# Marks issued with the similarity, self weights added on the diagonal, and SiLU as one ACT function in a two-stage image kernel

## The reference, cut to what matters

```python
xn  = xf / max(norm(xf), 1e-12)
sim = einsum('bnc,bmc->bnm', xn, xn)
val, idx = top_k(sim, 9)                       # the token itself is one of the nine
v   = val / (val.sum(-1) + 1e-06)
gcn = lambda feat, w, b: einsum('bnkc,bnk->bnc', (feat @ w)[idx], v) + b
out = silu(group_norm(gcn(xn, w1, b1)))        # 4 groups
out = silu(group_norm(gcn(out, w2, b2)))
x   = x + out
```

## Time and profile before

| | us |
|---|---|
| median of three runs | 780.92 |
| lowest, highest | 778.73, 781.6 |
| the profiled execution | 778.75 |
| its span, first to last instruction | 777.0 |
| PE busy | 663.6 (85%) |
| DVE busy | 574.1 (74%) |
| POOL busy | 483.0 (62%) |
| ACT busy | 353.3 (45%) |

### The profile page before, as it was taken

The page is one execution under the profiler, slowest core; times in us unless marked ns, Lnnn a source line. Parts: engine busy times, 40 slices in busy tenths (PEclk is TensorE's granted clock), DMA queues, the critical chain, the costliest instruction groups (busy, mean ns, idle before and its releaser), DMA issues.

```text
span 777.0 us, 11257 instructions
## 1 busy us (share of the span) xinstructions
PE 663.6 (85%) x3632; PEld 299.1 (38%) x3632; DVE 574.1 (74%) x1086; ACT 353.3 (45%) x578; POOL 483.0 (62%) x536
## 2 busy tenths in 40 slices
PE   3476869999999999999999999999999999787764
PEld 2353434444343434343434434343434343332221
DVE  2235678888888888888888878888888888866411
ACT  2234436364546555564546454646446454424110
POOL 0122665859596768676776849676767677674600
PEclk9557679999999999999999999999999999988776
DMA  2003242434343442524253434334353424333300
GB/s 68 1 14 56 54 96 54 96 57 95 82 96 68 81 97 56 121 57 109 56 95 68 96 69 96 77 81 88 64 106 64 90 60 83 74 83 75 69 14 14
DMA packets 148731, 55.93 MB, mean 72 GB/s; under 512 B 138017, under 2 KB 138273, under 8 KB 148673
## 3 DMA queue, kind: packets, MB, share of 16 engines
q1 hardware_dynamic: 148672, 55.21, 34.6%
HBM read 13.11 MB, written 4.33 MB: 22 GB/s over the span
## 4 chain that ended last, share of the span: by engine, by line
PE 51%; DVE 18%; issue 16%; POOL 8%; ACT 3%; DMA 2%; SPq 0%; POOLq 0%; ACTq 0%; DVEq 0%
PE pC L798 25%; PE pS L755 9%; DVE mask L603 5%; POOL rn L319 3%; DVE y L627 3%; PE pC L818 2%; PE pB L775 2%; PE pA L673 2%; POOL st_g L297 2%; DVE top L585 2%; PE pA L712 2%; PE pB L701 2%; PE pS L763 2%; ACT pB L464 1%; DVE st_g L497 1%
## 5 line engine op out<-in xcount | busy, mean ns | idle before, releaser
L798 PE MATMUL pC<-adj,xt 128*64 128x512 f32 x1024 | 265.4, 625 | 3.6 <-POOL adj L347 2.8
L585 DVE MAX8 top<-pS 128x8 f32<-128x1024 f32 x128 | 156.8, 1225 | 37.8 <-PE pS L763 36.6
L444 ACT COPY adj<-pS 128x1024 f32<-128x1024 f32 x128 | 129.2, 1009 | 95.1 <-PE pS L755 95.0
L347 POOL TENSOR_TENSOR adj<-maskT,adj 128x128 f32<-128x128 f16 (+7 forms) x128 | 164.4, 1285 | 11.7
L755 PE MATMUL pS<-xn 64*128 64x512 f32 x256 | 153.3, 682 | 10.9 <-DVE mask L603 5.7
L603 DVE MATCH_REPLACE8 mask<-top,pS 128x1024 uint16<-128x1024 f32 x128 | 155.4, 1214 | 0.0
L755 PE MATMUL pS<-xn,xsw 64*128 64x512 f32 x256 | 153.5, 682 | 2.0 <-DVE mask L603 1.8
L337 POOL TENSOR_TENSOR adj<-maskT,adj 128x128 f32<-128x128 f16 (+6 forms) x112 | 130.4, 1165 | 0.0
L798 PEld LDWEIGHTS pC<-adj,xt 128*64 128x64 f32 x1024 | 59.7, 139 | 88.8 <-issue 70.1
L319 POOL TENSOR_TENSOR rn<-ssq,minus_half 128x8 f32<-128x8 f32 x16 | 26.5, 1656 | 49.7 <-DVE selfsim L573 49.7
L613 DVE TENSOR_TENSOR g<-pC,vbc 128x512 f32<-128x512 f32 x32 | 22.1, 692 | 42.5 <-PE pC L798 42.5
(11 more groups left out here) (120 smaller groups left out, 1035.2 us busy)
## 6 DMA issues: line engine op xcount, KB each, us to landing
xs<-x SPq DMA_DIRECT2D x32, 128.0 KB, 2.8
rbc<-rn_row SPq DMA_DIRECT2D x32, 128.0 KB, 2.9
xsw<-xn SPq DMA_DIRECT2D x32, 128.0 KB, 2.5
vbc<-v_row SPq DMA_DIRECT2D x32, 128.0 KB, 2.9
out<-res SPq DMA_DIRECT2D x32, 128.0 KB, 2.4
maskT<-mask SPq DMA_TRANSPOSE x128, 3.1
cst<-packed SPq DMA_DIRECT2D x1, 453.5 KB, 3.5
rn_row<-rnT SPq DMA_DIRECT2D x16, 4.0 KB
```

The costliest lines, as they stand in the source:

```text
L347: pool.tensor_tensor(above, m[:, r, 0:r + 1, :].bitcast(F16), above, ALU.mult).then_inc(done["upper"], 1)
L444: act.copy(adj[b % 2][:, r, :], pS[r % 2][:, :]).then_inc(done["sim_copied"], 1)
L585: dve.max(top[:, r, :], pS[r % 2][:, :]).then_inc(done["tile_top"], 1)
L798: mm = pe.matmul(pC[h * C:(h + 1) * C, :], xt[:, t % NJ, t // NJ, :], adj[b % 2][:, t, h * H:(h + 1) * H], start=(t == 0), stop=(t == NT - 1))
```

## The change

- The two mark matmuls of a block stand directly behind its two similarity matmuls and in the same step; `marks` is gone as a stage. ACT copies the marked similarities, and MAX waits for the copy.
- The select on the diagonal is gone. The mask is zero there, so `upper` clears the diagonal, and POOL then adds `selves`, a diagonal of the tokens' own similarities, which ACT makes for each block from `ident` (new stage `itself`).
- `top` has ten columns: the eight largest, the own similarity and the small number. One reduce sums them. It is double-buffered.
- SiLU is one ACTIVATE with the function Silu, which writes `y2` or `y3` itself. `zh`, Tanh, L627 and the halved constants are gone, and with them Tanh's use of pB.
- The statistics of `g1` and `g2` use pB in place of pC. Their two matmuls stay.
- A new table of times, with a list `BEGINS` in place of `PERIOD`, sets another order on all queues.

```diff
-PERIOD = 41.68
+BEGINS = [0, 39.7423, 79.6495, 119.4031, 159.2975, 198.9522, 238.8737, 278.5581, 318.3809, 358.0611, 397.9632, 437.6484,
...
-                    live += [(b * PERIOD + at, steps) for at in TIMES[engine][stage.__name__]]
+                    live += [(BEGINS[b] + at, steps) for at in TIMES[engine][stage.__name__]]
...
-                    own = m[:, r, r, :].bitcast(F16)
-                    pool.affine_select(out=own, in_=own, compare_op=ALU.not_equal, fill=1.0, base=0, pattern=[[-1, P]],
-                                       channel_multiplier=1).then_inc(done["diagonal"], 1)
-                    if r == 0:
-                        pool.wait_ge(*of_tile("sim_copied", n))
-                    pool.wait_ge(*of_tile("diagonal", n))
+                    pool.wait_ge(*of_tile("sim_copied", n))
                     above = a[:, 0:r + 1, r * P:(r + 1) * P]
                     pool.tensor_tensor(above, m[:, r, 0:r + 1, :].bitcast(F16), above, ALU.mult).then_inc(done["upper"], 1)
+                    yield
+
+                    pool.wait_ge(*of_tile("upper", n))
+                    pool.wait_ge(*of_tile("self_ready", n))
+                    own = a[:, r, r * P:(r + 1) * P]
+                    pool.tensor_tensor(own, own, selves[:, r, :], ALU.add).then_inc(done["diagonal"], 1)
 
...
+            def itself(b):
+                for r in range(NT):
+                    yield
+                    act.wait_ge(*of("ss_read", b, 2))
+                    act.wait_ge(*of_tile("diagonal", NT * (b - 1) + r))
...
-            def silu_parts(b, tag, src, half):
+            def silu(b, tag, src, dst, signal):
                 yield
                 act.wait_ge(*of(f"{tag}_bias", b))
...
-                act.activation(pB[:, :], src[:, :], ACT.Tanh, bias=st[tag][:, 15:16],
...
+                if tag == "g1":
+                    act.wait_ge(*of("xt2_ps", b - 1))
+                else:
+                    act.wait_ge(*of("res_ready", b - 1))
+                act.activation(dst[:, :], src[:, :], ACT.Silu, bias=st[tag][:, 15:16], scale=st[tag][:, 14:15]).then_inc(done[signal], 1)
...
+                dve.wait_ge(*of("self_ready", b - 2, NT))
+                dve.wait_ge(*of("v_tot", b - 2))
 
                 dve.wait_ge(*of("ss_ps", b))
                 dve.tensor_scalar(ssq[:, :], pB[:, 0:NT], 1e-24, 1.0 / SSCALE, ALU.max, ALU.mult).then_inc(done["ss_read"], 1)
-                dve.tensor_scalar(selfsim[b % 2][:, :], pB[:, 0:NT], SSCALE * 1e24, SSCALE, ALU.mult, ALU.min).then_inc(done["ss_read"], 1)
+                dve.tensor_scalar(top[b % 2][:, :, TOP], pB[:, 0:NT], SSCALE * 1e24, SSCALE, ALU.mult, ALU.min).then_inc(done["ss_read"], 1)
...
-                    dve.wait_ge(*of_tile("marked", n))
-                    dve.wait_ge(*of("v_sum", b - 1))
-                    dve.max(top[:, r, :], pS[r % 2][:, :]).then_inc(done["tile_top"], 1)
+                    dve.wait_ge(*of_tile("sim_copied", n))
+                    dve.wait_ge(*of("v_tot", b - 2))
+                    dve.max(top[b % 2][:, r, 0:TOP], pS[r % 2][:, :]).then_inc(done["tile_top"], 1)
                 yield
                 dve.wait_ge(*of("tile_top", b, NT))
-                dve.tensor_reduce(vsum[:, :], top[:, :, :], AX.X, ALU.add).then_inc(done["v_sum"], 1)
-                dve.wait_ge(*of("v_sum", b))
                 dve.wait_ge(*of("ss_read", b, 2))
-                dve.scalar_tensor_tensor(out=vtot[:, :], in0=vsum[:, :], scalar=1e-6 * SSCALE, in1=selfsim[b % 2][:, :],
-                                         op0=ALU.add, op1=ALU.add).then_inc(done["v_tot"], 1)
...
-                variance(b, tag, pC)
-                yield
-                affine(b, tag, halved[:, first_const:first_const + 1], halved[:, first_const + 1:first_const + 2])
-                yield
-                dve.wait_ge(*of(f"{tag}_tanh", b))
-                if tag == "g1":
-                    dve.wait_ge(*of("xt2_ps", b - 1))
-                else:
-                    dve.wait_ge(*of("res_ready", b - 1))
-                dve.scalar_tensor_tensor(out=act_out[:, :], in0=pB[:, :], scalar=1.0, in1=half[:, :], op0=ALU.add,
-                                         op1=ALU.mult).then_inc(done[act_name], 1)
+                variance(b, tag, pB)
+                yield
+                affine(b, tag, const(weight), const(shift))
...
-                    mm = pe.matmul(pS[r % 2][:, h * H:(h + 1) * H], src[b % 2][c, rows], xn[b % 2][c, :], start=True, stop=True)
-                mm.then_inc(done["sim_ps"], 1)
-
-            def mark(b, r):
-                n = NT * b + r
-                own, _ = token_block(r)
-                pe.wait_ge(*of_tile("sim_copied", n))
+                    pe.matmul(pS[r % 2][:, h * H:(h + 1) * H], src[b % 2][c, rows], xn[b % 2][c, :], start=True, stop=True)
                 for s in range(2):
                     mm = pe.matmul(pS[r % 2][:, r * P + s * C:r * P + (s + 1) * C], place16[own, s, :], mark16[own, :], start=False,
                                    stop=True, skip_group_check=True)
-                mm.then_inc(done["marked"], 1)
+                mm.then_inc(done["sim_ps"], 1)
 
...
-                        pe.wait_ge(*of("upper", b, NT))
+                        pe.wait_ge(*of("diagonal", b, NT))
                         if signal == "g1_ps":
                             pe.wait_ge(*of("xt1_copied", b))
                             pe.wait_ge(*of("vT_copied", b))
-                            pe.wait_ge(*of("g2_veps", b - 1))
+                            pe.wait_ge(*of("vT_copied", b))
```

More of the change, by code:

```diff
@@ L289, in _ @@
             pool.memset(minus_half[:, :], -0.5).then_inc(done["prepared"], 1)
+            for p in range(2):
+                pool.memset(top[p][:, :, TOP + 1:TOP + 2], 1e-6 * SSCALE).then_inc(done["prepared"], 1)
             pool.memset(w1[:, :], 0.0).then_inc(done["prepared"], 1)
@@ L431, in unit @@
                 act.activation(sq[:, :], y1[:, :], ACT.Square).then_inc(done["sq_ready"], 1)
+            def itself(b):
[3 more added lines that the diff above has]
+                    act.wait_ge(*of_tile("diagonal", NT * (b - 1) + r))
+                    act.activation(selves[:, r, :], ident, ACT.Copy, scale=top[b % 2][:, r, TOP:TOP + 1]).then_inc(done["self_ready"], 1)
             def neighbours(b):
@@ L779, in neighbours @@
                     similarity(b, r)
-            def marks(b):
-                for r in range(NT):
-                    yield
-                    mark(b, r)
             def aggregate(b, xt, signal):
```

172 lines of the change are left out of this document (93 added, 79 removed).

## The result

| | before | changed |
|---|---|---|
| median, us | 780.34 | 722.73 |
| lowest, highest, us | 778.73, 781.6 | 721.89, 724.63 |
| span of the profiled execution, us | 777.0 | 721.3 |
| mean granted clock of TensorE | 0.921 | 0.933 |

The ratio is 0.9266, 95% interval 0.924 to 0.9292. The forecast was 749.0 us within 741 to 775: the sign was right, the gain was taken far too small (31.8 us, where the span shows 55.7).

A forecast was written before the change was run, and what follows sets the result against it. PE was taken as the bound, busy 38.98 of 41.66 us a period. Gains of 22.3 (twelve periods), 1.5 (fill), 1 (last period) and 7 (drain) sum to 31.8 us, giving 749 us, range 741 to 775.

The forecast's parts named there:

- the forecast's 1.4: Activations of a sample: one Silu replaces zh, Tanh and L627, so y2 and y3 come 1.4 us sooner.
- The first rival: Four table loads a period: a switch costs 1.28 us beyond its load, PE waits 3.8 us, 795 us; chance 0.12.
- PE's floor, "38.4": PE's work in a period, taken to fall to 38.4 us by 0.55 us of fewer joints.
- joints of the aggregate: Splits between groups of L798 matmuls: nine a period instead of four, 5 x 0.11 = 0.55 us less PE work.
- the walk round PE's order, "39.9": PE's new order followed once round from the first aggregate's end: 39.9 us; 39.8 taken, 1.86 us gained a period.
- the one for `xsw`: PE wants the swapped xn at 352.7, landing put at 351.7; rival of another wait keeping the period, 771 us, chance 0.09.
- the base: Twelve middle periods: gain of 1.86 us each counted from 41.66 us at full clock, 22.3 us in all.
- the ends: Outside the twelve periods: fill 1.5 us, period of the last sample 1 us, drain 7 us gained.
- at most 3.1 for the similarity: Drain: last similarity no longer behind xt2, masks and transposes up to 4 us sooner, of which 3.1 counted.

The follow-up runs named there:

- e1: Changed kernel with Tanh in place of Silu, so the table loads between Exp and Silu are gone: 721.13 us against 722.73.
- e3: Kernel before with only the mark matmuls put directly behind their similarity, old order, Tanh and select kept: 759.95 us.
- e6: Changed kernel without the two mark matmuls of each similarity: 718.21 us.
- e8: Changed kernel with each pair of mark matmuls one PE step behind its similarity instead of directly behind it: 758.78 us.
- e4: Kernel before with only Silu as one ACTIVATE and its four table loads a sample, old order: 776.57 us.
- e5: All parts of the change in the order of the kernel before, with the g1 and g2 statistics in pC: 783.1 us.
- e10: All parts in the old order, but ACT's st_in activations ahead of load and second Silu, three selves later: 764.24 us.
- e9: Changed kernel with one second-aggregate tile moved from behind the qn transposes to ahead of the next sample's first similarities: 726.31 us.

## Why the prediction was right in sign and wrong in size

**Right.** Silu is one ACTIVATE of 0.81 us, the value taken, and PE's wait for `y2` in the drain falls from 3.74 us to 2.35, by the forecast's 1.4:

```profile
699.00 2.07 PE L820 MATMUL pC<-w,y 128*128 128x128 f32 x8 [2.35 <-ACT y L463]
```

The loads take 1283 ns each, with the next ACTIVATE behind at once, and are hidden (e1). PE's waits for `y2` in the middle are gone. ACT comes to 28.0 us a period (27.6 said), POOL to 31.4 (31.2), DVE to 33.6 (33.7). None of them binds. An add on POOL took 0.457 us (0.432 taken), a `selves` on ACT 0.396 (0.266 taken). The first rival, a switch that costs more than its load, fell with the first row behind a load. The Trainium skill, page "ScalarE: Activation LUTs", section "What ACT_TABLE_LOAD costs", adds a drain of about 1380 ns to each load; this trace doesn't show it, with 1.30 us from the start of the load at 324.10 to that of the ACTIVATE.

**Wrong: PE's floor, "38.4".** I held that the marks change place only, "the same in number", and counted 0.55 us for joints of the aggregate. The same showed 0.16 us for a pair of marks, and I took that as its price anywhere. Behind a similarity it is 0.06 us: e3 has 1.17 us less PE work a period from the grouping alone, e6 prices the pair at 0.06, and e8, with the pair a step later, gives 0.8 us back. The new order takes another 37.81 - 37.20 = 0.6 us; longer runs of the aggregate's tiles fit it (twenty in a row 4.44 us, where five groups of four at the 1.01 of the earlier trace rows are 5.05), but no run had them alone. Together 1.78 us, where I had 0.55.

**Wrong: the walk round PE's order, "39.9".** It used 1.3 us for a similarity with its marks, though the earlier trace rows give 1.22 and the changed kernel 1.12: 8 x 0.18 = 1.4 us a round. That alone brings 39.9 to 38.5; measured are 38.96, since PE still idles 1.7 us a period, on waits for `qn` and `st_g`, which I had not named for the middle, and on the one for `xsw`, which I had. In all the periods are 0.84 us shorter than forecast, 10.1 us of the missing 23.9.

**Wrong: the base.** Twelve periods of before hold 3.3 us of lowered clock, and I took the gain per period from 41.66 without them. The changed kernel has no such period. Why the clock fell there stays open. It stayed up with the marks alone (e3), fell in six periods with the loads in the old order (e4, e5), and stayed up with `st_in` moved (e10). The amount of waiting doesn't order these: PE's waits between 200 and 600 us are 23.1 us in e4, 25.3 before, 28.4 in e3, 34.0 in e10 and 38.6 in e5.

**Wrong: the ends, 6.0, 3.5 and 10.5 us for 1.5, 1 and 7.** The fill gets no shorter in any kernel with the old order (130.9 to 132.6 us in e3, e4, e5 and e10), and is 124.6 to 128 in all with the new one, e8 apart: it comes with the new order, which I had said but not followed step by step. So does most of the last period's gain (38.65 us in e10, 36.20 in the changed kernel). The drain takes parts and order together: 97.6 us with the marks, 95.6 with Silu, 93.6 with all in the old order, 93.0 in the changed kernel. One thing that the term leaves out is the wait of 2.8 us that PE had for the last `upper` of a sample ahead of a first aggregate, which I had not looked for; the row in the trace of before is

```profile
736.57 8.86 PE L798 MATMUL pC<-adj,xt 128*64 128x512 f32 x32 [2.81 <-POOL adj L347]
```

and the changed kernel has no wait at its counterpart (683.31). It is gone with the marks alone: there PE waits 0.41 us at that place, for DVE, and the drain is 5.9 us shorter, where I had counted at most 3.1 for the similarity and nothing for the marks. How the 10.5 us divide among the parts isn't shown.

The three sizes together make the whole miss: 10.1 us of periods, 3.3 of base, 4.5 + 2.5 + 3.5 = 10.5 of ends, 23.9 in all.

**Left open.** What brings the clock down: waits of 0.93 us (ending at 256.49) and 1.17 us (ending at 259.81) let it stand at 2.4 GHz in the changed kernel, and behind 0.70 and 0.37 us it fell in some periods of e9 and not in others. How the 36 us of e8 divide among work, idle time and clock. How much of the order's gain belongs to the statistics in pB.

## What to carry to other kernels

Before counting an instruction at its row, ask what stands beside it there: a small matmul pair that PE comes back for cost 0.16 us, and directly behind its own similarity 0.06. A change of parts and a change of order are to be priced together: the same table loads cost 43 us in one order and nothing in the other, since what counts is what is queued behind them (`st_in`, `attn`, the Silu itself) and when PE asks for it. Where PE is busy nine tenths and more, read the granted clock of each period beside its waits: moving one step brought it down in three periods of twelve, at 3 us each, for 0.4 us gained in each of the others (e9).
